# Two-operand clamps on the vector engine, unit heads and square sums later in a slot, the rotary sum at a slot's end, and one layer norm of GpSimd a slot later

## The chip, the cores and the metric

The kernel runs on one NeuronCore of a Trainium2 chip. The metric is the device time of one launch in microseconds. A core has five engines that run at the same time, each with its own program in a fixed order: TensorE (PE, matrix products and transposes), VectorE (DVE), ScalarE (ACT), GpSimd (POOL) and SyncE (SP, which issues the DMA transfers here). They meet only at semaphores. PE writes its results to PSUM; POOL reads and writes SBUF alone.

## The reference, cut to what matters

There are 16 sequences of 512 tokens of width 128. Each goes through a first attention (16 heads of width 8, interleaved rotary, causal softmax) behind a layer norm, and then through a block of two layers with token shift, local attention (8 heads of width 64, windows of 64) and a gated MLP.

```
x = x + attn_ref(layernorm(x), wq, wk, wv, wo)
x = x + ffn_ref(layernorm(x), ...)
# each of the two layers in ffn_ref:
q = l2norm(q) * qs ; k = l2norm(k) * ksc      # t / clip(norm(t), 1e-12)
q, k = rotary_xpos(q, k)
o = local_attention(q, k, v) ; x = x + o @ wo
h = shift_token(x)
h = (h - mu) / sqrt(var + 1e-05) * lg + lb
a, g = split(h @ w1 + b1) ; x = x + (a * gelu(g)) @ w2 + b2
```

The clip of the norm is the clamp that the change touches: the kernel takes the maximum of the sum of squares and 1e-24 and then raises it to the power -0.5. The other clamp-like step is the addition of 1e-5 to a variance.

## The kernel before, in words

**Rounds and slots.** Two sequences ("lanes") are a pair, and there are 8 pairs. A round `i` has 16 slots `s`. In a slot the five engines work on a tile of 128 tokens of the two-layer block (`ITEMS` = 2 layers x 2 lanes x 4 tiles = 16 per round, so 128 tiles in all), on two heads of the first attention of a later pair, and on small parts of two other stages: the projections of the pair after next ("next") in slots 0 to 6 for one lane and 8 to 14 for the other, and the end of the first attention of the next pair ("first"). The program is written out slot by slot: rounds -2 and -1 fill the pipeline (no tiles of the block), rounds 0 to 5 hold everything, round 6 has no "next" stage, round 7 has tiles only, and a short tail follows. Every engine's list of one slot is the `for s in slots` loop at the end of its section; nothing reorders it.

**One tile.** PE projects q and k, three slots ahead (`project_qk(s + 3)`, L699). ACT copies them to `RAW` and squares them (`SQ`). DVE sums the squares per head and clamps the sum: `norms(s + 3)`, L1029 and L1032, in place in `ss`. POOL raises `ss` to the power -0.5 (`over_norms(s + 2)`, L1408, result `inv`), multiplies `RAW` by the rotary tables (L1386, and L1397 twice) and adds the two (`added`, L1403). DVE multiplies by `inv`: `unit_heads(s + 1)`, L1012, result `QN`. PE turns `QN` (`turn_qk`), computes the scores of tile `s` (L725 is their first product, so it marks the start of a slot on PE), DVE takes the maxima (L1019, L1022), ACT the exponentials, PE the values (L751), DVE divides by the sums (`over_sums(s)`, L1036 and L1039, result `ON`), PE merges with `wo` (L786), DVE adds to the stream `Z` (`add_heads(s - 1)`, L1048), and `tile_moments(s - 1)` ends with L1066, the variance plus 1e-5 (`veps`), from which POOL takes the root (L1378) and normalises (L1417).

**Waits between DVE and POOL.** `over_norms(s + 2)` waits for `unit_heads(s + 1)` of the same slot (`qn_ready`), because `RC` and `inv` are single buffers. `norms(s + 3)` waits for `over_norms(s + 2)` of the same slot (`inv_ready`), because `ss` is a single buffer. `scores(s + 1)` on PE waits for `ON` of tile `s`.

**Six steps of the first attention.** In each slot PE, DVE and ACT pass six `attention_step`s (positions 0 to 5), for two heads of three chunks. DVE takes row maxima (L977). The bank of PSUM is single, so PE's scores of step n (L587) wait for DVE's maximum of step n - 1: what stands between two steps on DVE can hold up PE.

**The MLP.** In even slots DVE multiplies the gates (`gate_up`, L1076), PE projects down (L828), DVE adds (`add_mlp`, L1084), and in the second layer also adds the kept input (`XR`, L1089). In slots 4, 6, 8 and 10 PE then turns the result (`turn_half`), which waits for L1084.

**POOL's other work.** At the start of an even slot it splits the maxima (`maxima_parts`, L1367 to L1373), for which PE's L622 waits in that slot. `next_normalise` (L1348, L1342) stands at the start of slots 1 and 9, ahead of `over_norms`. `first_normalise` (L1354, L1342) of lane 1 stands at the start of slot 15, that of lane 0 at the end of slot 7. SP reloads `X1` (`load_first`) once the latter is through.

Of the kernel before, what the change touches and what calls it, by code (L numbers as in the profile page):

```python
# [21 lines left out]
P = 128  # L22
B, S, D = 16, 512, 128
NT = S // P
# [146 lines left out]
def build(nc, t, out):  # L171
    with ExitStack() as ctx:
# [28 lines left out]
        lgb = sb("lgb", [P, L, 2])  # L201
        nhalf = sb("nhalf", [P, 2 * H2])
        spare = sb("spare", [P, 1])
        unit1 = sb("unit1", [P, 1])
# [183 lines left out]
        N_FIRST, N_CONST = 4, 10 + L * 7  # L388
        N_MADE = LANES + 9

# [7 lines left out]
        def _(sp):  # L398
# [31 lines left out]
            def body(i, slots):  # L430
# [69 lines left out]
                for s in slots:  # L500
# [11 lines left out]
                    for z in range(LANES):  # L512
# [4 lines left out]
                        if s == 7 + 8 * z and lives(i, 1):  # L517
                            keep_first(1, z)
                    if s == 8 and lives(i, 1):
                        sp.wait_ge(*past(ln_out.sem[0], ln_out.at(later(i, 1), 1)))  # L520
                        load_first(1, 1)
# [394 lines left out]
        def _(v):  # L916
# [3 lines left out]
            def moments(k, z, src, to, counted, meant, done):  # L920
                stats, mv, veps = to
                for tt in range(NT):
                    ins = v.bn_stats(stats[:, tt, :], src[:, tt, :])
                ins.then_inc(counted.sem[z], 1)
                v.wait_ge(*past(counted.sem[z], counted.at(k, 1)))
                v.tensor_copy(spare[:, 0:1], nhalf[:, 0:1])
                for tt in range(NT):
                    ins = v.bn_aggr(mv[:, tt, :], stats[:, tt, :])
                ins.then_inc(meant.sem[z], 1)
                v.wait_ge(*past(meant.sem[z], meant.at(k, 1)))  # L930
                v.tensor_scalar(veps[:, :], mv[:, :, 1], EPS, None, ALU.add).then_inc(done.sem[z], 1)

# [10 lines left out]
            def next_sin(n, z, w):  # L943
                if w:
                    v.wait_ge(*past(parts.sem[z], parts.at(n, w)))
                v.wait_ge(*past(proj.sem[z], proj.at(n, 2 * w + 2)))
                v.tensor_tensor(rope_s[:, :], a_ps, sin1[:, :], ALU.mult).then_inc(roped.sem[z], 1)
                v.wait_ge(*past(roped.sem[z], roped.at(n, 2 * w + 2)))
                v.tensor_tensor(rope_t[:, :], rope_t[:, :], rope_s[:, :], ALU.add).then_inc(rope_sum.sem[z], 1)
# [20 lines left out]
            def body(i, slots):  # L970
# [55 lines left out]
                def norms(m):  # L1026
                    v.wait_ge(*past(sq_done.sem, sq_done.at(i, m + 1)))
                    v.wait_ge(*past(inv_ready.sem, inv_ready.at(i, m)))
                    v.tensor_reduce(ss[:, :], SQ.rearrange("p (h e) -> p h e", e=E2), AX.X,  # L1029
                                    ALU.add).then_inc(ss_sum.sem, 1)  # L1030
                    v.wait_ge(*past(ss_sum.sem, ss_sum.at(i, m + 1)))
                    v.tensor_scalar(ss[:, :], ss[:, :], 1e-24, None, ALU.max).then_inc(ss_ready.sem, 1)  # L1032

# [26 lines left out]
                def tile_moments(m):  # L1060
# [4 lines left out]
                    v.wait_ge(*past(tile_mean.sem, tile_mean.at(i, m + 1)))  # L1065
                    v.tensor_scalar(veps[z][:, tt:tt + 1], mv[z][:, tt, 1:2], EPS, None,  # L1066
                                    ALU.add).then_inc(tile_var.sem, 1)
# [23 lines left out]
                for s in slots:  # L1091
# [4 lines left out]
                    if isinstance(i, int) and i == -2 and s == 7:  # L1096
                        scale_tables()
                    if tile_in(i, s):
                        maxima(s)
                    attention_step(s, 0)  # L1100
                    if tile_in(i, s + 1):
                        unit_heads(s + 1)
                    if s % 8 == 4 and lives(i, 2):
                        next_cos(two, z, 1)
                        next_low(two, z, 0)
                    if s % 8 == 6 and lives(i, 2):
                        next_low(two, z, 1)
                    attention_step(s, 1)
                    if tile_in(i, s - 1):
                        add_heads(s - 1)  # L1110
                    attention_step(s, 2)
                    if s % 8 == 3 and lives(i, 2):
# [5 lines left out]
                    attention_step(s, 3)  # L1118
                    if tile_in(i, s + 3):
                        norms(s + 3)  # L1120
                    if tile_in(i, s - 1):
                        shifted_tokens(s - 1)
                    if b:
                        gate_up(p, 0)
                        gate_up(p, 1)
                    if s % 2 and unit_in(i, (s + 17) // 2):
                        heads_over_sum((s + 17) // 2)
                    if tile_in(i, s - 1):
                        tile_moments(s - 1)
# [14 lines left out]
                    if s % 8 == 2 and lives(i, 2):  # L1144
                        next_sin(two, z, 0)
                    if s % 8 == 6 and lives(i, 1):
                        add_attention(one, z)
# [178 lines left out]
        def _(g):  # L1326
# [8 lines left out]
            g.memset(unit1[:, :], 1.0).then_inc(made, 1)  # L1335
            g.memset(nhalf[:, :], -0.5).then_inc(made, 1)
            g.wait_ge(made, N_MADE)

# [20 lines left out]
            def body(i, slots):  # L1359
# [62 lines left out]
                for s in slots:  # L1422
# [16 lines left out]
                    if tile_in(i, s - 1):  # L1439
                        tile_normalise(s - 1)  # L1440
                    if s == 7 and lives(i, 1):
                        first_normalise(later(i, 1), 0)
# [73 lines left out]
```

## Time and profile before

| | |
|---|---|
| Median of 3 runs | 2443.89 us (2443.87 to 2459.32) |
| Profiled execution | 2439.99 us, of which the span is 2438.2 us |
| PE, matrix products | busy 2153.6 us (88%) |
| DVE | busy 1763.4 us (72%) |
| ACT | busy 1553.0 us (64%) |
| POOL | busy 1773.9 us (73%) |
| DMA | 49 GB/s over the span |

How to read it: busy is the time in which an engine has at least one instruction under way. Matrix products overlap each other, so a busy PE can hold waits that don't show as idle. No engine is near the whole span, so the order of the lists and the waits between them decide, and the trace of waits and the timeline are of more use than the shares. Times in the rows are microseconds from the start of the span unless marked ns.

### The profile page before, as it was taken

The numbers are of one execution on the slowest core, as the hardware profiler recorded it, in microseconds if no ns is written. First come the engines' busy times: TensorE is split into PE (matmuls) and PEld (weight loads), VectorE is DVE, ScalarE is ACT, GpSimd is POOL, SyncE is SP. The second block draws the span as 40 slices with busy tenths as digits, with TensorE's granted clock in tenths as the row PEclk, the third lists the DMA queues.
The fourth block names the chain that finished last, engine by engine and source line by source line (L and its number), as shares of the span: only waits on it lengthen the run. The fifth ranks groups of instructions, "written<-read, shape, count | busy, mean of one in ns | idle before, by whom it ended". The sixth has DMA issues, their size and how long they took to land.

```text
span 2438.2 us, 55022 instructions
## 1 busy us (share of the span) xinstructions
PE 2153.6 (88%) x20736; PEld 1447.8 (59%) x20736; DVE 1763.4 (72%) x4632; ACT 1553.0 (64%) x2510; POOL 1773.9 (73%) x1615
## 2 busy tenths in 40 slices
PE   4887899899999989998999999999899999988886
PEld 1444566665666666665666656666566666665654
DVE  4766777787777877788777777778777777666653
ACT  1445666676676667666766766766676667765553
POOL 2126768787777868787686777878787778788882
PEclk9999999999999999999999999999999999999997
DMA  4222121121212111121112112121121211111110
GB/s 138 65 66 54 40 53 49 44 59 45 57 37 60 52 46 49 48 59 46 49 49 59 44 45 58 33 64 51 39 51 47 60 48 36 25 32 27 28 25 23
DMA packets 115081, 119.56 MB, mean 49 GB/s; under 512 B 31945, under 2 KB 88054, under 8 KB 114818
## 3 DMA queue, kind: packets, MB, share of 16 engines
q1 hardware_dynamic: 114818, 116.04, 18.2%
q8 instruction: 167, 2.74, 0.5%
q14 instruction: 96, 0.79, 0.1%
HBM read 55.96 MB, written 20.97 MB: 32 GB/s over the span
## 4 chain that ended last, share of the span: by engine, by line
PE 38%; DVE 21%; ACT 14%; POOL 13%; issue 11%; DMA 1%; SPq 1%; ACTq 0%; DVEq 0%; POOLq 0%
PE ps L734 4%; PE ps L645 4%; POOL inv L1408 4%; DVE ps L977 4%; PE ps L554 4%; PE ps L828 3%; DVE nm L1019 3%; PE ps L587 3%; DVE ss L1029 3%; PE ps L712 3%; PE ps L600 2%; PE ps L567 2%; ACT PT L1190 2%; PE ps L810 2%; PE ps L819 2%
## 5 line engine op out<-in xcount | busy, mean ns | idle before, releaser
L977 DVE CUSTOM_DVE_ANT_0 ps<-ps,causal 128x512 f32<-128x512 f32 (+3 forms) x1024 | 492.4, 506 | 328.3 <-PE ps L587 322.3
L1408 POOL TENSOR_TENSOR inv<-ss,nhalf 128x16 f32<-128x16 f32 x128 | 377.7, 2950 | 394.0 <-DVE QN L1012 394.0
L1190 ACT ACTIVATE PT<-ps 128x512 f32<-128x512 f32 (+1 forms) x768 | 409.1, 536 | 352.5 <-PE ps L602 349.8
L587 PE MATMUL ps<-KA,QA 72*128 72x512 bf16 (+3 forms) x1024 | 275.1, 311 | 77.1 <-DVE nmax L977 72.9
L1397 POOL TENSOR_TENSOR RS<-RAW,rot 128x512 f32<-128x512 f32 x256 | 319.9, 1271 | 0.0
L1403 POOL TENSOR_TENSOR RC<-RC,RS 128x1024 f32<-128x1024 f32 x128 | 300.9, 2351 | 18.4
L600 PE MATMUL ps<-QA,KA 75*128 75x512 bf16 (+3 forms) x1024 | 286.8, 306 | 27.8 <-ACT PT L1190 26.0
L1386 POOL TENSOR_TENSOR RC<-RAW,rot 128x1024 f32<-128x1024 f32 x128 | 307.9, 2405 | 0.0
L1019 DVE TENSOR_REDUCE nm<-ps 128x8 f32<-128x1024 f32 x128 | 156.4, 1222 | 119.3 <-PE ps L734 119.3
L699 PE MATMUL ps<-wqkv,ZT 128*128 128x512 f32 x512 | 241.9, 595 | 0.0
L587 PEld LDWEIGHTS ps<-KA,QA 72*128 72x128 bf16 x1024 | 96.4, 100 | 235.3 <-DVE nmax L977 142.4
L1249 ACT COPY V_odd<-ps 128x512 f32<-128x512 f32 x128 | 75.0, 586 | 233.6 <-PE ps L712 232.1
L1029 DVE TENSOR_REDUCE ss<-SQ 128x16 f32<-128x1024 f32 x128 | 155.7, 1217 | 72.5 <-POOL inv L1408 65.5
L602 PE MATMUL ps<-causal_t,identb 128*128 128x128 bf16 x1024 | 200.9, 222 | 0.0
L1225 ACT ACTIVATE PX<-PX 128x1024 f32<-128x1024 f32 x128 | 136.5, 1067 | 54.8 <-DVE PX L1022 54.1
L600 PEld LDWEIGHTS ps<-QA,KA 75*128 75x128 bf16 x1024 | 101.0, 99 | 115.8 <-ACT PT L1190 64.7
L645 PE MATMUL ps<-PT,V 128*32 128x512 f32 (+3 forms) x2048 | 153.4, 440 | 9.1 <-DVE X L1003 2.9
L1022 DVE TENSOR_TENSOR PX<-ps,nm 128x1024 f32<-128x1024 f32 x128 | 156.7, 1224 | 4.4
L1012 DVE TENSOR_TENSOR QN<-RC,inv 128x1024 f32<-128x1024 f32 x128 | 156.5, 1223 | 0.0
L828 PE MATMUL ps<-w,G 128*128 128x128 f32 (+1 forms) x768 | 110.8, 297 | 44.8 <-DVE G L1076 44.8
L734 PEld LDWEIGHTS ps<-KT,QT 64*64 64x64 f32 x4096 | 114.3, 136 | 56.7 <-issue 56.7
L751 PE MATMUL ps<-V_even,PT 128*64 128x65 f32 x2048 | 147.2, 225 | 0.4
(122 smaller groups left out, 5304.9 us busy)
## 6 DMA issues: line engine op xcount, KB each, us to landing
V_even<-V_odd SPq DMA_DIRECT2D x256, 130.0 KB, 2.6
QA<-parts SPq DMA_DIRECT2D x192, 96.0 KB
KA<-parts SPq DMA_DIRECT2D x192, 96.0 KB
parts<-qkp SPq DMA_DIRECT2D x32, 384.0 KB, 3.5
X_next<-in_x SPq DMA_DIRECT2D x16, 256.0 KB, 3.1
X<-in_x SPq DMA_DIRECT2D x16, 256.0 KB, 2.9
x_kept<-X SPq DMA_DIRECT2D x16, 256.0 KB, 3.8
XR<-x_kept SPq DMA_DIRECT2D x32, 128.0 KB, 2.9
```

Of the source, the lines that this page charges most:

```text
L587: last = pe.matmul(dst[:, c0:c0 + w], QA[e][0:QK_ROWS, h % UNIT, qt * P:(qt + 1) * P], KA[e][0:QK_ROWS, h % UNIT, 0:w], start=True, stop=True)
L600: pe.matmul(dst[:, c0:c0 + w], KA[e][0:ROWS, h % UNIT, kt * P:(kt + 1) * P], QA[e][0:ROWS, h % UNIT, kt * P:S], start=True, stop=False)
L645: last = pe.matmul(a_ps[32 * n:32 * (n + 1), kt * P:S], V1[z][:, kt, h * VW:h * VW + 32], PT1[:, n, c0:c0 + w], start=(kt == 0), stop=(kt ...
L699: mm = pe.matmul(ps[:, w, :], ZT[z][:, tt * P:(tt + 1) * P], wqkv[:, l, w * INNER:(w + 1) * INNER], start=True, stop=True)
L977: ins = v.tensor_tensor_reduce(for_max(i, x)[:, c0:c0 + w], for_max(i, x)[:, c0:c0 + w], causal[:, S - w:S], -1.0, -NEG, ALU.add, ALU.min, ...
L1019: v.tensor_reduce(nm[:, :], blocks, AX.X, ALU.max, negate=True).then_inc(max_ready.sem, 1)
L1029: v.tensor_reduce(ss[:, :], SQ.rearrange("p (h e) -> p h e", e=E2), AX.X, ALU.add).then_inc(ss_sum.sem, 1)
L1190: a.activation(PT1[:, h % UNIT, c0:c0 + w], for_exp(i, x)[:, 0:w], ACT.Exp, scale=SCALE1).then_inc(exped.sem, 1)
L1386: g.tensor_tensor(RC.rearrange(heads, w=2, h=H2), RAW[m % 2].rearrange(heads, w=2, h=H2), rot[:, l, tt, 0, :, :].unsqueeze(2).to_broadcast ...
L1397: ins = g.tensor_tensor(turned[:, w, :, :, :], by_half[:, w, :, :, :], table[:, w, :, :].unsqueeze(1).to_broadcast([P, H2, 2, E2 // 2]), A ...
L1403: g.tensor_tensor(RC, RC, RS, ALU.add).then_inc(added.sem, 1)
L1408: g.tensor_tensor(inv[:, :], ss[:, :], nhalf[:, :], ALU.pow).then_inc(inv_ready.sem, 1)
```

## The change

**Two operands instead of a constant.** Two small tables are filled once by POOL: `tiny` (1e-24, 128x16) and `eps` (1e-5, 128x4). The clamp L1032 and the additions of 1e-5 (L1066, L931) were `tensor_scalar` with a constant; they are `tensor_tensor` with the table as the second operand.

**Order of DVE's list.** `unit_heads(s + 1)` moves from behind step 0 to behind step 1 and `add_heads`. `norms(s + 3)` moves from behind step 3 to behind the gates and `heads_over_sum`. `shifted_tokens` moves with it. In slots 4 and 12 the product by the cosines (`next_cos`, lane w = 1) moves to the very start of the slot and `next_low` behind step 2. The sum of the two rotary products (L949) is a function of its own, at the end of slots 2, 4, 10 and 12; in slots 4 and 12 it stood right behind the product by the sines.

**POOL and SP.** `first_normalise` of lane 0 moves from the end of slot 7 to the end of slot 8, and SP's reload of `X1` from slot 8 to slot 10.

```diff
-                v.tensor_scalar(veps[:, :], mv[:, :, 1], EPS, None, ALU.add).then_inc(done.sem[z], 1)
+                v.tensor_tensor(veps[:, :], mv[:, :, 1], eps[:, :], ALU.add).then_inc(done.sem[z], 1)
...
                 v.tensor_tensor(rope_s[:, :], a_ps, sin1[:, :], ALU.mult).then_inc(roped.sem[z], 1)
+
+            def next_sum(n, z, w):
                 v.wait_ge(*past(roped.sem[z], roped.at(n, 2 * w + 2)))
...
-                    v.tensor_scalar(ss[:, :], ss[:, :], 1e-24, None, ALU.max).then_inc(ss_ready.sem, 1)
+                    v.tensor_tensor(ss[:, :], ss[:, :], tiny[:, :], ALU.max).then_inc(ss_ready.sem, 1)
...
-                    v.tensor_scalar(veps[z][:, tt:tt + 1], mv[z][:, tt, 1:2], EPS, None,
+                    v.tensor_tensor(veps[z][:, tt:tt + 1], mv[z][:, tt, 1:2], eps[:, 0:1],
...
+                    if s % 8 == 4 and lives(i, 2):
+                        next_cos(two, z, 1)
                     if tile_in(i, s):
                         maxima(s)
                     attention_step(s, 0)
+                    attention_step(s, 1)
+                    if tile_in(i, s - 1):
+                        add_heads(s - 1)
                     if tile_in(i, s + 1):
                         unit_heads(s + 1)
+                    attention_step(s, 2)
                     if s % 8 == 4 and lives(i, 2):
-                        next_cos(two, z, 1)
                         next_low(two, z, 0)
                     if s % 8 == 6 and lives(i, 2):
                         next_low(two, z, 1)
-                    attention_step(s, 1)
-                    if tile_in(i, s - 1):
-                        add_heads(s - 1)
-                    attention_step(s, 2)
...
-                    if tile_in(i, s + 3):
-                        norms(s + 3)
-                    if tile_in(i, s - 1):
-                        shifted_tokens(s - 1)
                     if b:
                         gate_up(p, 0)
                         gate_up(p, 1)
                     if s % 2 and unit_in(i, (s + 17) // 2):
                         heads_over_sum((s + 17) // 2)
+                    if tile_in(i, s + 3):
+                        norms(s + 3)
+                    if tile_in(i, s - 1):
+                        shifted_tokens(s - 1)
...
                         next_sin(two, z, 0)
+                        next_sum(two, z, 0)
+                    if s % 8 == 4 and lives(i, 2):
+                        next_sum(two, z, 1)
...
-                    if s == 7 and lives(i, 1):
+                    if s == 8 and lives(i, 1):
                         first_normalise(later(i, 1), 0)
```

The rows below show three places in the programs of both kernels, all in round 2. Behind the edits the changed kernel's line numbers are 2 to 10 higher (L977 is L981 there, L1012 is L1016, L1408 is L1418); the second row of each L977 reads the accumulator.

DVE, slot 10, from step 0 on, before:

```order
L977 ISA ps,nmax<-ps,causal 128x512
L977 ISA nmax 128x1
L1012 TENSOR_TENSOR QN<-RC,inv 128x1024
L977 ISA ps,nmax<-ps,causal 128x384
L977 ISA nmax 128x1
L977 ISA ps,nmax<-ps,causal 128x128
L977 ISA nmax 128x1
L1048 TENSOR_TENSOR Z<-ps,Z 128x128
```

The same place in the changed kernel:

```order
L981 ISA ps,nmax<-ps,causal 128x512
L981 ISA nmax 128x1
L981 ISA ps,nmax<-ps,causal 128x384
L981 ISA nmax 128x1
L981 ISA ps,nmax<-ps,causal 128x128
L981 ISA nmax 128x1
L1052 TENSOR_TENSOR Z<-ps,Z 128x128
L1016 TENSOR_TENSOR QN<-RC,inv 128x1024
```

`QN` stood behind the first maximum and now stands behind the next two (step 1 has two) and behind the addition to `Z`.

DVE, slot 10, from step 3 to `veps`, before:

```order
L977 ISA ps,nmax<-ps,causal 128x512
L977 ISA nmax 128x1
L1029 TENSOR_REDUCE ss<-SQ 128x16
L1032 TENSOR_SCALAR ss<-ss 128x16
L1058 BN_STATS stats<-XN 128x6
L1076 SCALAR_TENSOR_TENSOR G<-ps,b,G 128x256 x2
L1063 COPY spare<-nhalf 128x1
L1064 BN_AGGR mv<-stats 128x2
L1066 TENSOR_SCALAR veps<-mv 128x1
```

The same place in the changed kernel:

```order
L981 ISA ps,nmax<-ps,causal 128x512
L981 ISA nmax 128x1
L1080 SCALAR_TENSOR_TENSOR G<-ps,b,G 128x256 x2
L1033 TENSOR_REDUCE ss<-SQ 128x16
L1036 TENSOR_TENSOR ss<-ss,tiny 128x16
L1062 BN_STATS stats<-XN 128x6
L1067 COPY spare<-nhalf 128x1
L1068 BN_AGGR mv<-stats 128x2
L1070 TENSOR_TENSOR veps<-mv,eps 128x1
```

The gates come first now, then the sum of squares and the clamp, which reads a second tensor, then the moments, whose last row reads a second tensor too.

POOL, from the end of slot 7 to the start of slot 8's `inv`, before:

```order
L1378 TENSOR_TENSOR rstd<-veps,nhalf 128x1
L1414 TENSOR_TENSOR pool_spare<-nhalf 128x1
L1417 TENSOR_SCALAR XN<-Z,mv,rstd 128x64
L1417 TENSOR_SCALAR XN<-XN,mv,rstd 128x64
L1354 TENSOR_TENSOR first_rstd<-first_veps,nhalf 128x4
L1340 TENSOR_TENSOR pool_spare<-nhalf 128x1
L1342 TENSOR_SCALAR Z_first<-X,first_mv,first_rstd 128x128 x4
L1367 TENSOR_TENSOR nparts<-nmax,unit 128x4x4
L1369 TENSOR_TENSOR nres<-nmax,nparts 128x4x4
L1371 TENSOR_TENSOR nparts<-nres,unit 128x4x4
L1373 TENSOR_TENSOR nparts<-nres,nparts 128x4x4
L1408 TENSOR_TENSOR inv<-ss,nhalf 128x16
```

The changed kernel, from the end of slot 8 to slot 9's `inv`:

```order
L1388 TENSOR_TENSOR rstd<-veps,nhalf 128x1
L1424 TENSOR_TENSOR pool_spare<-nhalf 128x1
L1427 TENSOR_SCALAR XN<-Z,mv,rstd 128x64
L1427 TENSOR_SCALAR XN<-XN,mv,rstd 128x64
L1364 TENSOR_TENSOR first_rstd<-first_veps,nhalf 128x4
L1350 TENSOR_TENSOR pool_spare<-nhalf 128x1
L1352 TENSOR_SCALAR Z_first<-X,first_mv,first_rstd 128x128 x4
L1358 TENSOR_TENSOR rstd_next<-veps_next,nhalf 128x4
L1350 TENSOR_TENSOR pool_spare<-nhalf 128x1
L1352 TENSOR_SCALAR XN_next<-X_next,mv_next,rstd_next 128x128 x4
L1418 TENSOR_TENSOR inv<-ss,nhalf 128x16
```

The layer norm into `Z_first` now stands directly ahead of the one into `XN_next`, both ahead of slot 9's `inv`; in slot 8 `nparts` no longer has it in front.

## Rows read from the trace of the kernel before

**Rows 1.** Waits of all engines: engine, line, releaser, us in total, times, longest:

```profile
POOL inv L1408 <- DVE QN L1012: 394.0, 92, 8.6
...
PEld ps L587 <- DVE nmax L977: 142.4, 145, 4.7
...
DVE ss L1029 <- POOL inv L1408: 65.5, 34, 5.4
...
PE ps L828 <- DVE G L1076: 44.8, 40, 3.8
...
PE ps L622 <- POOL nparts L1373: 17.7, 10, 4.0
```

**Rows 2.** Groups of instructions, the clamp: busy us, mean ns; idle before:

```profile
L1032 DVE TENSOR_SCALAR ss<-ss 128x16 f32<-128x16 f32 x128 | 119.3, 932 | 4.4
```

**Rows 3.** Single lines of DVE: duration ns min/median/max, first and last start:

```profile
L1032 DVE TENSOR_SCALAR ss<-ss x128: 175/878/3462, 192.8 to 2364.7; 128x16 f32<-128x16 f32 x128
...
L949 DVE TENSOR_TENSOR rope_t<-rope_t,rope_s x32: 691/693/2332, 23.5 to 1870.2; 128x512 f32<-128x512 f32 x32
...
L1066 DVE TENSOR_SCALAR veps<-mv x128: 153/154/156, 252.8 to 2418.1; 128x1 f32<-128x1 f32 x128
```

**Rows 4.** Timeline of slot 4, DVE and POOL: start us, duration us, instruction:

```profile
871.53 2.33 DVE L949 TENSOR_TENSOR rope_t<-rope_t,rope_s 128x512 f32<-128x512 f32 x1
...
870.96 2.35 POOL L1403 TENSOR_TENSOR RC<-RC,RS 128x1024 f32<-128x1024 f32 x1
```

**Rows 5.** Timeline, DVE and POOL, a product beside the power and L1386:

```profile
318.58 0.69 DVE L953 TENSOR_TENSOR rope_s<-rope_t,qkp 128x512 f32<-128x512 f32 x1
...
316.00 2.92 POOL L1408 TENSOR_TENSOR inv<-ss,nhalf 128x16 f32<-128x16 f32 x1 [8.53 <-DVE QN L1012]
318.89 2.60 POOL L1386 TENSOR_TENSOR RC<-RAW,rot 128x1024 f32<-128x1024 f32 x1
```

**Rows 6.** Timeline of round 2, PE: starts of slots 0, 1 and 8 to 11:

```profile
788.02 0.38 PE L725 MATMUL ps<-band,identb 128*128 128x512 bf16 x1
...
802.92 0.59 PE L725 MATMUL ps<-band,identb 128*128 128x512 bf16 x2
...
929.47 0.59 PE L725 MATMUL ps<-band,identb 128*128 128x512 bf16 x2
...
946.93 0.59 PE L725 MATMUL ps<-band,identb 128*128 128x512 bf16 x2
...
964.41 0.59 PE L725 MATMUL ps<-band,identb 128*128 128x512 bf16 x2
...
980.84 0.59 PE L725 MATMUL ps<-band,identb 128*128 128x512 bf16 x2
```

**Rows 7.** Timeline of slot 10, DVE, then POOL:

```profile
969.11 1.22 DVE L1012 TENSOR_TENSOR QN<-RC,inv 128x1024 f32<-128x1024 f32 x1
...
971.09 0.29 DVE L1048 TENSOR_TENSOR Z<-ps,Z 128x128 f32<-128x128 f32 x1
...
974.24 1.22 DVE L1029 TENSOR_REDUCE ss<-SQ 128x16 f32<-128x1024 f32 x1
975.49 0.27 DVE L1032 TENSOR_SCALAR ss<-ss 128x16 f32<-128x16 f32 x1
...
978.50 0.69 DVE L1039 TENSOR_TENSOR ON<-ps,rec 128x512 f32<-128x512 f32 x1
...
970.47 2.92 POOL L1408 TENSOR_TENSOR inv<-ss,nhalf 128x16 f32<-128x16 f32 x1 [2.07 <-DVE QN L1012]
973.36 2.36 POOL L1386 TENSOR_TENSOR RC<-RAW,rot 128x1024 f32<-128x1024 f32 x1
975.69 2.50 POOL L1397 TENSOR_TENSOR RS<-RAW,rot 128x512 f32<-128x512 f32 x2
```

**Rows 8.** Timeline of POOL in slot 9, the next pair's layer norm ahead of `inv`:

```profile
949.94 1.03 POOL L1348 TENSOR_TENSOR rstd_next<-veps_next,nhalf 128x4 f32<-128x4 f32 x1
...
955.23 2.92 POOL L1408 TENSOR_TENSOR inv<-ss,nhalf 128x16 f32<-128x16 f32 x1
```

More of the change, by code:

```diff
@@ L202, in build @@
         nhalf = sb("nhalf", [P, 2 * H2])
+        tiny = sb("tiny", [P, 2 * H2])
+        eps = sb("eps", [P, NT])
         spare = sb("spare", [P, 1])
@@ L388, in build @@
         N_FIRST, N_CONST = 4, 10 + L * 7
-        N_MADE = LANES + 9
+        N_MADE = 2 * LANES + 9
         def past(sem, value):
@@ L518, in body @@
                             keep_first(1, z)
-                    if s == 8 and lives(i, 1):
+                    if s == 10 and lives(i, 1):
                         sp.wait_ge(*past(ln_out.sem[0], ln_out.at(later(i, 1), 1)))
@@ L1336, in _ @@
             g.memset(nhalf[:, :], -0.5).then_inc(made, 1)
+            g.memset(tiny[:, :], 1e-24).then_inc(made, 1)
+            g.memset(eps[:, :], EPS).then_inc(made, 1)
             g.wait_ge(made, N_MADE)
```

## The prediction

> **What bounds the kernel now.** I read the waits first. PE waits for DVE in two places: its scores L587 for the row maxima L977 (142.4 us on the weight side), and its down projection L828 for the gates (44.8 us) [rows 1]. DVE waits for POOL's power `inv` 34 times (65.5 us), and POOL waits 394.0 us for DVE's `QN` [rows 1]. So POOL has air (some 3 us per slot) and starts each tile only when DVE says so; DVE is late at some places and early at others; PE carries most of the span. Then the groups and the single lines: DVE's clamp L1032 of 16 columns takes 932 ns on average, 119.3 us in all [rows 2], but 175 ns at its shortest and 3462 ns at its longest [rows 3]. The work is the same each time, so the rest, 119 - 128 x 0.175 = 97 us, is waiting inside the instruction. The timeline says for what. In slot 10 the clamp ran from 975.49 to 975.76 and POOL's L1386 from 973.36 to 975.72 [rows 7]: it ended 0.04 us behind POOL's instruction. L1066 does almost the same on one column and never takes more than 156 ns [rows 3].
>
> **Does a two-operand form escape that wait?** This decides the case. The trace has no clamp with two tensors, but it has L949, a sum of two f32 tensors in SBUF: 691 ns at best, 2332 at worst [rows 3]. One of 2.33 us began at 871.53, 0.57 us into POOL's L1403, which ended at 873.31; L949 ended at 873.86 [rows 4], 0.55 behind it, so it did its 0.69 us of work only from about 0.14 before POOL's end on. With 0.175 us of work and the same start, a two-tensor clamp would end 0.035 behind POOL's instruction, just where the one-tensor clamp ends now. The other bound is L953, also two SBUF tensors (one bf16), which took its plain 0.69 us beside L1408; but L1408 is the power, and the next L1386, which met the end of L953, took 2.60 us instead of 2.36 [rows 5, 7]. So between 0 and -97 us of DVE time for L1032, I take 0: the POOL instructions that it meets are L1386 and L1397, products like L1403 and not powers. And L1066, which now never waits, becomes a two-tensor instruction. It follows 0.45 us behind L1032, when POOL runs L1397: cost 0 if it stays exempt, up to one L1397 (1.25 us) if not. I take that it waits.
>
> The Trainium skill says the same more sharply ("SBUF — State Buffer", section "Who interferes with whom"): a DVE instruction with two SBUF inputs contends with a GpSimd instruction that reads SBUF. By it the clamp gains nothing and L1066 loses. Rows 4 agree with it.
>
> **The moved steps.** What counts is how late `QN` becomes, since `inv` waits for `QN`, the sum of squares waits for `inv`, and on DVE's list the clamp, `veps`, step 4, `ON` and with it PE's next slot stand behind the sum of squares.
>
> In slot 10 before: `QN` ends at 970.33, `inv` runs 970.47 to 973.39, L1029 starts at 974.24 (0.85 of slack), `ON` ends at 979.19, PE starts slot 11 at 980.84 [rows 6, 7]. After: `QN` stands behind L1048, which waits for PE's merge and ends at 971.38. `QN` ends at 972.5, 2.2 later. From there the chain is:
> - `inv`: 0.15 + 2.92;
> - L1029, 0.05 behind `inv`: 1.22. The clamp then meets L1386 (2.36) and ends with it, 2.39 behind the end of `inv`;
> - 0.45 of moments; `veps` meets the first L1397 (1.25) and ends with it, 3.65 behind the end of `inv`;
> - the two maxima of step 4, 0.75 and, in slots 2 and 10, 0.6 of L941; `ON`: 0.2 + 0.7.
>
> Sum 0.15 + 2.92 + 3.65 + 0.75 + 0.95 = 8.4 from the end of `QN` to `ON`. `QN` ends 972.5 - 964.4 = 8.1 behind PE's slot start, so an even slot lasts at least 16.5 to 16.6 us, an odd one (its `QN` comes some 1.6 later, behind PE's values) at least 18.2. Before, slot 0 lasted 802.92 - 788.02 = 14.9, slot 10 16.4, slot 8 17.46, slot 9 17.48 [rows 6].
>
> Per round, in us, by that floor: slot 0 +1.7; slot 2 +0.9; slot 10 +1.5 (with L941 and the turn behind `add_mlp`, 0.9); odd slot 7 +1.1; slots 3, 5, 11, 13 are long already and change by 0. Slots 4 and 12 gain: today L957, L941 and `QN` hold up step 1, and L949's stretch (2.33, of which 1.64 is waiting [rows 3, 4]) holds up step 4. Both go; the floor takes the rest of it: -1.0 and -1.3. In slots 6 and 14 the gates no longer wait for the clamp: +0.1 and -0.7. Slot 1 loses its 3.46 us clamp but sits on the floor: -0.9.
>
> **POOL's layer norm.** In slot 8 it no longer stands ahead of `nparts`, for which PE waits about 2 us there (17.7 us in ten waits [rows 1]); but slot 8's floor (16.6 + 0.9) equals its 17.46 of today: 0. In slot 9 the two norms come back to back. One costs 955.23 - 949.94 = 5.3 us [rows 8]. POOL is done with slot 8 at 949.9 as today (its `QN` was POOL-bound there), then 4.5 and 4.5 to 5.4 more: `inv` starts at about 959.5 instead of 955.2, `ON` ends about 8.3 later, and PE starts slot 10 at 967.9 instead of 964.41: +3.5. Slot 15 has a norm ahead of `inv` behind a slot 14 that now ends later on POOL: +1.9. DMAs: SP issues the same ones, the reload of `X1` two slots later is needed only in slot 14 and landed in about 3 us; nothing.
>
> Sum per round: 1.7 - 0.9 + 0.9 - 1.0 + 0.1 + 1.1 + 0 + 3.5 + 1.5 - 1.3 - 0.7 + 1.9 = +6.8, times six full rounds = +41. Round 6 has shorter slots: +1.6 on most even ones, less slot 8, +1.1 on six odd ones: +13. Round 7: the gates, for which L828 waits there (44.8 us in all [rows 1]), come earlier, but the same chain ends even slots where they end now (+0.2 each), odd ones +1.1: +10. Total +64 on 2440 of the profiled execution, 2504; that execution is 4 us below the median of the runs, and I round to **2500**.
>
> **Rivals.**
> 1. *The two-tensor forms don't wait at all* (small tensors, as L953 beside the power). Then the clamp saves 0.8 to 1.0 and `veps` costs nothing: the chain is 1.7 shorter. Slots 0, 2, 7, 10 come back to 0, slots 4 and 12 gain about 3 each, 6 and 14 1.3 each, 1 gains 1.7, 8 gains 1.6, 9 still loses 3.7, 15 is even: about -8 per round, -48, and some -12 behind: **2380**. For it: nothing in the trace but rows 5. This one is on the other side. It decides as soon as the chain from `QN` to `ON` is under 6.8 us.
> 2. *L1032 waits, the one-column L1066 stays exempt*, as its one-column form is now. The chain is 0.8 shorter; that lifts some 12 slots of a full round and 15 each of the last two: 64 - 6 x 9.6 - 24 = -18, about **2425**, and with the slack left in some of these slots anything up to 2460. No difference that counts.
> 3. *DVE loses its turn.* Where the clamp began just behind `inv`, with about 1 us of L1386 left, POOL's next product sometimes went first, three times in a row (the 3462 ns [rows 3]; it happened 7 times, nearly all in slot 1). After the change nearly every clamp begins at that phase. If one in five is lost, 128 x 0.2 x 2.2 = +56 more: **2560**.
>
> **Chances.** The forecast 0.45, rival 1 0.17, rival 2 0.23, rival 3 0.15. About 1% (24 us) is what a measurement of this kernel can tell from none. Slower by over 1%: 0.45 + 0.15 = 0.60; faster: rival 1 and a part of rival 2, 0.20; between: 0.20. The forecast's own range is 2470 to 2540, the whole 2405 to 2560, which leaves out most of rival 1 and the far end of rival 3.
>
> **What would show it.** L1032's mean stays near or above 0.9 us (rival 1: 0.18). L1066's mean goes from 0.154 to 0.5 or more (rival 2: stays). DVE's wait for `inv` grows well over 65.5 us, and DVE gets a busy time near today's or above. PE starts slot 10 of round 2 over 3 us later after slot 9 began than now. L949's maximum falls to about 0.7. I am wrong if the clamp is short beside L1386, or if DVE reaches the sum of squares behind the end of `inv` in most slots.

## The result, and the profile after

The changed kernel took 2500.61 us (median of 4 runs, 2497.22 to 2522.69), the kernel before 2447.55 us (4 runs). The ratio is 1.0225, with a 95% interval of 1.0182 to 1.0268: slower by about 2%; the medians are 53 us apart. The prediction said 2500 and slower.

The page of the changed kernel, its span and busy times (us, share, number of instructions):

```profile
span 2495.9 us, 55024 instructions
...
PE 2172.9 (87%) x20736; PEld 1438.3 (58%) x20736; DVE 1860.5 (75%) x4632; ACT 1550.4 (62%) x2510; POOL 1740.5 (70%) x1617
```

DVE is busy for 97 us more with exactly as many instructions. Its waits (engine, line, releaser: us in total, times, longest):

```profile
POOL inv L1418 <- DVE QN L1016: 510.3, 119, 8.6
...
PEld ps L589 <- DVE nmax L981: 179.6, 234, 7.4
...
DVE ss L1033 <- POOL inv L1418: 91.9, 78, 6.0
```

Against [rows 1], POOL waits 116 us more for `QN`, 119 times instead of 92; DVE waits for `inv` 78 times instead of 34; and PE's score products wait for DVE's maxima 37 us more. The single lines of DVE in the changed kernel (duration in ns, min/median/max):

```profile
L1036 DVE TENSOR_TENSOR ss<-ss,tiny x128: 176/1011/3455, 184.4 to 2428.3; 128x16 f32<-128x16 f32 x128
...
L1070 DVE TENSOR_TENSOR veps<-mv,eps x128: 158/733/1991, 243.8 to 2476.9; 128x1 f32<-128x1 f32 x128
...
L953 DVE TENSOR_TENSOR rope_t<-rope_t,rope_s x32: 677/692/1114, 23.0 to 1912.2; 128x512 f32<-128x512 f32 x32
```

The clamp got no shorter (median 1011 ns, 878 in [rows 3]). The step that never waited, 154 ns in [rows 3], now takes 733. The rotary sum lost its 2.33 us stretch: at most 1.11 us now.

The timeline of slot 10 of round 2 in the changed kernel (start us, duration us; in brackets the idle time before and what ended it), the place of [rows 7]. DVE, then POOL:

```profile
983.70 1.22 DVE L1016 TENSOR_TENSOR QN<-RC,inv 128x1024 f32<-128x1024 f32 x1
...
988.09 1.22 DVE L1033 TENSOR_REDUCE ss<-SQ 128x16 f32<-128x1024 f32 x1 [0.71 <-POOL inv L1418]
989.34 1.03 DVE L1036 TENSOR_TENSOR ss<-ss,tiny 128x16 f32<-128x16 f32 x1
...
990.85 0.73 DVE L1070 TENSOR_TENSOR veps<-mv,eps 128x1 f32<-128x1 f32 x1
...
993.05 0.69 DVE L1043 TENSOR_TENSOR ON<-ps,rec 128x512 f32<-128x512 f32 x1
...
985.06 2.92 POOL L1418 TENSOR_TENSOR inv<-ss,nhalf 128x16 f32<-128x16 f32 x1 [3.29 <-DVE QN L1016]
987.95 2.39 POOL L1396 TENSOR_TENSOR RC<-RAW,rot 128x1024 f32<-128x1024 f32 x1
990.28 2.51 POOL L1407 TENSOR_TENSOR RS<-RAW,rot 128x512 f32<-128x512 f32 x2
```

The clamp ends at 990.37, 0.03 behind L1396 (990.34). The row of L1407 holds two products; `veps` ends at 991.58, behind the first of them. `QN` ends at 984.92 and `ON` at 993.74: the chain is 8.8 us long. DVE now stands idle 0.71 us before the sum of squares, where before it came 0.85 late.

The granted clock by slot, PE alone (stretch in us, its length, PE busy and its instructions, granted clock, DMA share, GB/s). Slots 1, 9 and 10 of round 2 before the change:

```profile
802.92:822.37 19.45, 17.40 (x177) 1.00 0.27 66
...
946.93:964.40 17.47, 16.99 (x176) 1.00 0.14 33
964.40:980.84 16.44, 15.93 (x153) 1.00 0.24 66
```

The same slots in the changed kernel, then slot 9 of round 3, then slot 1 of round 1:

```profile
810.60:830.33 19.73, 18.95 (x175) 0.91 0.17 39
...
956.42:976.81 20.39, 18.37 (x177) 0.94 0.12 32
976.81:994.69 17.88, 16.27 (x152) 1.00 0.26 70
...
1246.85:1272.06 25.21, 17.79 (x177) 0.88 0.17 46
...
518.61:537.37 18.76, 17.26 (x175) 1.00 0.18 42
```

Where the 58 us between the two profiled executions (2438.2 and 2495.9 us) lie, by PE's slot starts: up to the first slot of round 0 -9; rounds 0 to 5 +47; round 6 +19; round 7 with the tail +1.

### The profile page after: what moved, and what is told of

Read it like the earlier page. It is cut to its first block, busy times and chain, and to the rows that moved or that the text cites. A ratio compares the mean times of both kernels' runs of the same rounds, so it can differ in the third digit from the quotient of the medians.

```text
span 2495.9 us, 55024 instructions
## 1 busy us (share of the span) xinstructions
PE 2172.9 (87%) x20736; PEld 1438.3 (58%) x20736; DVE 1860.5 (75%) x4632; ACT 1550.4 (62%) x2510; POOL 1740.5 (70%) x1617
## 3 DMA queue, kind: packets, MB, share of 16 engines
q1 hardware_dynamic: 114818, 116.04, 17.3%
## 4 chain that ended last, share of the span: by engine, by line
PE 33%; DVE 31%; POOL 17%; ACT 10%; issue 8%; DMA 1%; SPq 1%; DVEq 0%; POOLq 0%; ACTq 0%
POOL inv L1418 12%; PE ps L736 5%; PE ps L647 5%; DVE ss L1033 5%; DVE QN L1016 5%; DVE ps L981 5%; DVE ss L1036 4%; PE ps L788 4%; PE ps L701 3%; PE ps L589 3%; DVE nm L1023 3%; DVE PX L1026 3%; PE ps L727 3%; PE ps L556 2%; PE ps L602 2%
## 5 line engine op out<-in xcount | busy, mean ns | idle before, releaser
L1418 POOL TENSOR_TENSOR inv<-ss,nhalf 128x16 f32<-128x16 f32 x128 | 374.4, 2925 | 510.3 <-DVE QN L1016 510.3
L981 DVE CUSTOM_DVE_ANT_0 ps<-ps,causal 128x512 f32<-128x512 f32 (+3 forms) x1024 | 490.2, 503 | 198.0 <-PE ps L589 195.8
L1407 POOL TENSOR_TENSOR RS<-RAW,rot 128x512 f32<-128x512 f32 x256 | 319.2, 1270 | 0.0
L1413 POOL TENSOR_TENSOR RC<-RC,RS 128x1024 f32<-128x1024 f32 x128 | 302.2, 2361 | 18.6 <-POOL RS L1407 0.4
L1396 POOL TENSOR_TENSOR RC<-RAW,rot 128x1024 f32<-128x1024 f32 x128 | 303.0, 2367 | 0.0
L647 PE MATMUL ps<-PT,V 128*32 128x512 f32 (+3 forms) x2048 | 159.8, 454 | 24.4 <-issue 15.7
L1016 DVE TENSOR_TENSOR QN<-RC,inv 128x1024 f32<-128x1024 f32 x128 | 155.5, 1215 | 0.2 <-issue 0.2
L736 PEld LDWEIGHTS ps<-KT,QT 64*64 64x64 f32 x4096 | 120.5, 142 | 58.3 <-issue 58.3
L736 PE MATMUL ps<-KT,QT 64*64 64x128 f32 x4096 | 153.9, 292 | 0.0
```

Of the source, the lines that this page charges most:

```text
L647: last = pe.matmul(a_ps[32 * n:32 * (n + 1), kt * P:S], V1[z][:, kt, h * VW:h * VW + 32], PT1[:, n, c0:c0 + w], start=(kt == 0), stop=(kt ...
L736: mm = pe.matmul(ps[b * WIN:(b + 1) * WIN, 2 + s, j * P:(j + 1) * P], QT[half, j, b * WIN:(b + 1) * WIN], keys, start=False, stop=j == PAI ...
L981: ins = v.tensor_tensor_reduce(for_max(i, x)[:, c0:c0 + w], for_max(i, x)[:, c0:c0 + w], causal[:, S - w:S], -1.0, -NEG, ALU.add, ALU.min, ...
L1396: g.tensor_tensor(RC.rearrange(heads, w=2, h=H2), RAW[m % 2].rearrange(heads, w=2, h=H2), rot[:, l, tt, 0, :, :].unsqueeze(2).to_broadcast ...
L1407: ins = g.tensor_tensor(turned[:, w, :, :, :], by_half[:, w, :, :, :], table[:, w, :, :].unsqueeze(1).to_broadcast([P, H2, 2, E2 // 2]), A ...
L1413: g.tensor_tensor(RC, RC, RS, ALU.add).then_inc(added.sem, 1)
```

## The experiments

Ratios are to the kernel before on the same chip, timed in the same session (2435.9 to 2437.0 us there). Kernels of different sessions are compared by their ratios: so the changed kernel's 1.0225 against e5's 1.0040 is 1.85%, 45 us. The two intervals together leave some 12 us on either side of such a difference. "Per round" is the mean of rounds 2 to 5 of the profiled execution: 284.9 us before, 292.7 changed.

**e1, the changed kernel with constants again** (all three lines; the cut shows two, one of them without the line that it replaces).

```diff
-                    v.tensor_tensor(ss[:, :], ss[:, :], tiny[:, :], ALU.max).then_inc(ss_ready.sem, 1)
+                    v.tensor_scalar(ss[:, :], ss[:, :], 1e-24, None, ALU.max).then_inc(ss_ready.sem, 1)
...
+                    v.tensor_scalar(veps[z][:, tt:tt + 1], mv[z][:, tt, 1:2], EPS, None,
```

> The changed kernel with the constant forms back (clamp and both additions of 1e-5), all moves kept. Theory A (late inv with waits): the clamp stays at about 1.0 us, since the constant form waits for POOL's product just as the two-operand form does; the one-column addition falls from 0.73 to 0.15 us, which shortens the chain from QN to ON by 0.58 in some 12 slots of a full round: 12 x 0.58 x 6 = 42 us, with round 6 about 50, so about 2450. Theory B (only the moves count): 2500.

2442.06 us, ratio 1.0032 [1.0013, 1.0051]; per round 286.7. Nearly the whole loss is gone, and the clamp's row reads as in the changed kernel:

```profile
L1036 DVE TENSOR_SCALAR ss<-ss x128: 174/1006/3433, 187.1 to 2375.9; 128x16 f32<-128x16 f32 x128
```

**e5, only `veps` back on a constant.**

> The changed kernel with only the per-tile variance step (veps, 128x1) back on a constant; the clamp keeps its two operands. Theory A (what the two-operand forms cost is almost all in the one-column veps, held up beside POOL's L1407 in every slot; the clamp waits the same either way): veps back to 0.154 us, 128 x 0.58 us shorter on the chain, ratio to the kernel before 1.003 +- 0.005 as in e1_constants, about 2445 us, clamp mean still near 1.04 us. Theory B (the two-operand clamp costs too, by lost turns or a longer hold): about half way, ratio 1.012, 2470 us.

2443.27 us, ratio 1.0040 [1.0015, 1.0066], equal to e1 within their intervals (8 us). So the two-operand clamp costs and saves nothing that shows; the one-column step carries the loss, some 45 us. In its row of the e5 kernel it takes its own time again:

```profile
L1070 DVE TENSOR_SCALAR veps<-mv x128: 153/154/155, 247.2 to 2442.7; 128x1 f32<-128x1 f32 x128
```

Most of the slots that got shorter in e1 and e5 lost 0.6 us, but slots 3 and 15 got 0.6 and 0.8 longer. The addition to `XR` (L1093) at the end of the slots before them has two SBUF inputs as well. When it begins earlier, it waits longer for the end of POOL's sum L1413: ahead of slot 15 of round 2 it ended 0.28 us behind that in the changed kernel and 0.29 in e1. Its row in the changed kernel, then in e1:

```profile
L1093 DVE TENSOR_TENSOR XR<-XR,Z x32: 424/1394/1987, 447.4 to 2493.2; 128x256 f32<-128x256 f32 x32
...
L1093 DVE TENSOR_TENSOR XR<-XR,Z x32: 425/1986/2601, 451.3 to 2437.7; 128x256 f32<-128x256 f32 x32
```

**e2, the kernel before with the two-operand forms alone.**

> The kernel before with the two-operand forms only, no move. Theory A: the clamp keeps its mean of about 0.93 us; the one-column addition finds POOL's product with 0.08 us left in even slots (nothing) and 0.37 left in odd ones (0.24 us more), so within 10 us of before, 2445 to 2458. If the operand forms alone were the cause: about 2500. If two operands escaped the wait: clamp 0.18 us and a faster kernel.

2471.96 us, ratio 1.0135 [1.0066, 1.0205]: a miss, 36 us where under 10 were expected. The four runs fall into two groups, 2458 to 2460 and 2484 to 2487 us (+22 to +51); the profiled one (2484.10) belongs to the upper, so what follows tells of that. In the order of before `veps` comes when POOL's second L1397 (L1401 here) has little left, so it takes 0.38 us at the median. But the clamp sometimes begins while POOL's L1390 (L1386 before) is under way and comes back only behind POOL's next two products. I call that a lost turn. There were 11 in this execution and 7 before, and each now costs twice, since `veps` then meets the sum L1407 (1.63 to 1.65 us behind each of the 11). Timeline of e2, slot 1 of round 2, DVE, then POOL:

```profile
827.60 3.47 DVE L1034 TENSOR_TENSOR ss<-ss,tiny 128x16 f32<-128x16 f32 x1
...
831.90 1.64 DVE L1068 TENSOR_TENSOR veps<-mv,eps 128x1 f32<-128x1 f32 x1
...
826.21 2.37 POOL L1390 TENSOR_TENSOR RC<-RAW,rot 128x1024 f32<-128x1024 f32 x1
828.55 2.49 POOL L1401 TENSOR_TENSOR RS<-RAW,rot 128x512 f32<-128x512 f32 x2
831.18 2.34 POOL L1407 TENSOR_TENSOR RC<-RC,RS 128x1024 f32<-128x1024 f32 x1
```

The clamp ends 0.03 behind the second L1401, and `veps` 0.02 behind L1407. Slot 1 grew by 1.7 us, slot 2 behind it by 1.0 (its clock in round 2 was 0.93).

**e3, `unit_heads` back behind step 0 in the changed kernel.**

```diff
                     attention_step(s, 0)
+                    if tile_in(i, s + 1):
+                        unit_heads(s + 1)
                     attention_step(s, 1)
                     if tile_in(i, s - 1):
                         add_heads(s - 1)
-                    if tile_in(i, s + 1):
-                        unit_heads(s + 1)
```

> The changed kernel with unit_heads back behind step 0, all else kept. Theory A: inv starts 2 to 3 us earlier, so DVE no longer waits for it in slots 0, 2, 7, 10 and those of round 6: the sum of squares starts off the phase right behind inv. 4 to 5 us per full round and 15 in round 6 come back: 2450 to 2465. If the lateness of QN does not matter: 2500.

2436.32 us, ratio 1.0006 [0.9981, 1.0031]; per round 285.6. The direction was right, the size larger than expected: undoing this edit alone also takes away the whole loss, 53 us by the ratios. The full rounds gave 7 us each for the 4 to 5 expected, round 6 12 for 15, and round 7 with the tail 20 for nothing.

**e9, the kernel before with `unit_heads` later and nothing else.**

> The kernel before with unit_heads behind step 1 and add_heads as its only edit. Theory A (the prediction's chain: QN some 2 us later makes inv, the sum of squares and ON later in most slots; e3_heads_back won 7 us per round by undoing it): +4 to +7 us per round, less in slots 4 and 12 where the rotary steps hold PE up anyway; 2465 to 2485 us, ratio 1.012 to 1.020. Theory B (it costs only together with the held veps): ratio under 1.005, 2445 us.

2579.98 us, ratio 1.0578 [1.0540, 1.0615]. Both theories were far too small: 143 us. The waits of e9 name what both had left out:

```profile
DVE ss L1029 <- POOL inv L1408: 207.6, 119, 5.1
PEld ps L828 <- DVE G L1076: 141.2, 63, 4.2
```

In the order of before the gates stand behind the sum of squares. When `QN` is late, so is `inv`; DVE stops at the sum of squares, and the gates stop with it. Slot 10 of round 2 in e9, DVE:

```profile
1026.56 1.22 DVE L1029 TENSOR_REDUCE ss<-SQ 128x16 f32<-128x1024 f32 x1 [1.44 <-POOL inv L1408]
...
1028.87 0.85 DVE L1076 SCALAR_TENSOR_TENSOR G<-ps,b,G 128x256 f32<-128x256 f32 x2
```

Behind that wait PE's clock falls. The same slot of e9, PE, in its last four stretches of 2 us, and the slot as a whole:

```profile
1027.00:1029.00 2.00, 0.99 (x32) 1.00 0.15 51
1029.00:1031.00 2.00, 1.23 (x11) 1.00 0.46 111
1031.00:1033.00 2.00, 2.00 (x7) 0.56 0.35 119
1033.00:1035.00 2.00, 2.00 (x7) 0.58 0.07 22
...
1015.28:1035.13 19.85, 17.56 (x151) 0.91 0.22 59
```

The slot took 16.44 us before, with PE busy for 15.93. Of the 3.4 us that it grew, 1.6 are PE's busy time, the same work at the lower level of its clock. Round 4 shows the price by itself: the wait for the gates was the same 1.78 us, the clock stayed at 1.00, and the slot took 18.15 us:

```profile
1615.40:1633.55 18.15, 15.85 (x152) 1.00 0.24 62
```

Slot 8 has a second wait. With the later `QN` POOL reaches the layer norm at the end of slot 7 later, and PE waits 4.1 us for `nparts`, 1.9 before. The changed kernel has neither wait: PE waited for the gates only at the very end (0.97 us, twice) and in slot 8 of no full round for `nparts`. So the new place of the gates and that of the layer norm take away what makes the later `QN` so dear in e9. No run has the later `QN` with one of the two alone, so how the difference divides between them is not shown.

**e4, the kernel before with the rotary moves alone** (`next_cos` first, `next_low` behind step 2, the sum at the slot's end).

> The kernel before with the rotary moves only (product by the cosines first in slots 4 and 12, residual low parts behind step 2, sum at the slot's end). Theory A: slots 4 and 12 lose the 1.64 us wait of the sum and the hold-up of step 1 (about 1.1), slots 6 and 14 about 0.6: 4 to 5 us per full round, 2415 to 2425. If those waits were covered: 2447.

2368.89 us, ratio 0.9732 [0.9695, 0.9770]; per round 273.7, 11.2 less where 4 to 5 were expected. Slots 4 and 12 went from 19.3 and 18.6 us to 15.7 and 15.8, 6 and 14 from 17.6 and 17.3 to 16.0 and 15.8, and slot 1 lost 2.0, since its clamp lost its turn in one round of six instead of in all of them. In each of these four even slots PE is idle for only 0.5 us now.

**e7, e4 with the sum of squares and `shifted_tokens` behind the gates.**

> The kernel before with the rotary moves of e4_rotary_only and, in addition, the sum of squares and clamp behind the gates. Theory A (the later sum of squares costs nothing, since the sum of squares waits for inv anyway, and PE's wait for the gates in slots 0 and 8, 0.65 and 0.87 us, goes): -1 to -1.5 us per round against e4_rotary_only, about 2360 us, ratio 0.970. Theory B (each 0.9 us by which the clamp is later makes the next slot's inv and ON late): +6 or more per round, 2400 us or more, ratio 0.985 or more.

2365.19 us, ratio 0.9719 [0.9695, 0.9743]. That can't be told from e4; theory B falls. It holds two opposite things: full rounds are 2.0 us longer (in slot 8 PE waits 0.7 to 1.2 us for `Z`), and round 7 with the tail is 14 us shorter (233.4 for 247.5), where the gates come earlier.

**e6, the layer norm back in slot 7 of the changed kernel.**

> The changed kernel with the first layer norm of lane 0 back at the end of slot 7 and SP's reload of X1 back in slot 8. Theory A (slot 9's 21.7 us comes from two layer norms back to back ahead of inv): slot 9 falls to about 18, slot 8 gets PE's wait for nparts back (about 1.9 us, before it 1.0 of its floor), sum -2 to -3 per round, about 2480 us, ratio 1.013 to 1.017. Theory B (slot 9 is long because QN comes late anyway): slot 9 stays over 20.5 us, 2495 to 2505 us, ratio 1.022.

2525.95 us, ratio 1.0376 [1.0348, 1.0404]. Slot 9 got shorter, as theory A said (3.3 us), but the sum has the other sign, so neither theory holds. The slots 8 and 9 of round 2 in e6, and POOL in slot 8:

```profile
953.47:976.18 22.71, 16.12 (x146) 0.92 0.22 59
976.18:994.26 18.08, 17.30 (x176) 1.00 0.07 17
```

```profile
958.68 3.74 POOL L1352 TENSOR_SCALAR Z_first<-X,first_mv,first_rstd 128x128 f32<-128x128 f32 x4
962.39 0.21 POOL L1377 TENSOR_TENSOR nparts<-nmax,unit 128x16 bf16<-128x16 f32 x1
```

With the later `QN` POOL reaches the norm later, so PE's wait for `nparts` is 3.5 us instead of the 1.9 before, and slot 8 lasts 22.7 us, against 17.5 with the norm moved (where PE never waits for `nparts`). Moving it takes 5.2 us out of slot 8 and puts 3.3 into slot 9. Of the 26 us between the two profiled spans 14 lie in rounds 0 to 5, 5 in round 6 and 5 before round 0; by the ratios it is 37 us.

**e8, e4 with a clamp that takes one SBUF operand.** The maximum is a reduction over pairs (sum, 1e-24); the result is the same.

```diff
-                    v.tensor_reduce(ss[:, :], SQ.rearrange("p (h e) -> p h e", e=E2), AX.X,
+                    v.tensor_reduce(pair[:, :, 0], SQ.rearrange("p (h e) -> p h e", e=E2), AX.X,
...
-                    v.tensor_scalar(ss[:, :], ss[:, :], 1e-24, None, ALU.max).then_inc(ss_ready.sem, 1)
+                    v.tensor_reduce(ss[:, :], pair[:, :, :], AX.X, ALU.max).then_inc(ss_ready.sem, 1)
```

> e4_rotary_only with the clamp written as a maximum over pairs (sum, 1e-24) by a tensor_reduce, that is one SBUF input of 128x32 and no constant; same result. Theory A (what holds the clamp is the kind of operand access, and an instruction with one plain SBUF input runs beside POOL's product): the clamp takes its own 0.2 us in all 128 tiles instead of 0.77 on average, no lost turns; since even slots of e4_rotary_only have no stall left, it gives time in slots 9, 13 and 15 and in the last two rounds, 2345 to 2360 us, ratio 0.963 to 0.970. Theory B (anything DVE starts there waits for POOL's product): clamp mean stays near 0.77, 2369 us, ratio 0.973.

2353.07 us, ratio 0.9668 [0.9648, 0.9688]. The clamp in e8, and in slot 10 beside POOL's L1394 (L1386 before), DVE, then POOL:

```profile
L1035 DVE TENSOR_REDUCE ss<-pair x128: 185/186/189, 189.9 to 2282.3; 128x16 f32<-128x32 f32 x128
```

```profile
945.04 0.19 DVE L1035 TENSOR_REDUCE ss<-pair 128x16 f32<-128x32 f32 x1
...
942.91 2.37 POOL L1394 TENSOR_TENSOR RC<-RAW,rot 128x1024 f32<-128x1024 f32 x1
```

It began 0.24 us before POOL's product ended and did not wait for it, and in no tile took over 0.189 us. Theory A holds: the kind of instruction decides, not the moment. It is 0.6% under e4, its interval just clear of e4's; e10 prices the clamp more clearly.

**e10, this clamp as the only edit of the kernel before.**

> The kernel before with the pair clamp of e8_pair_clamp as its only edit. It prices a clamp that never waits. Theory A (of the 97 us of waiting in the clamp only the lost turns, 3.46 us in slot 1, and some in slots 8 and 15 lie on the path): clamp 0.186 us in all tiles, slot 1 down by 1 to 2 us, the other slots by under 0.5, -2 to -3.5 us per round, 2415 to 2425 us, ratio 0.990 to 0.995. Theory B (rival 1 of the prediction: most of it is on the path): 2390 us or less, ratio 0.98 or less.

2397.54 us, ratio 0.9834 [0.9811, 0.9857]: 39 us, between the two theories. Slot 1 gave 1.5 us, slots 6, 14 and 15 0.9 each (in slot 15 all of it is one lost turn, in round 3), and round 7 with the tail 12 (242.6 for 254.4): there the clamp had waited 0.8 us in each of 13 tiles, 10.5 us together, so about all of it lay on the path.

**e11, e8 with the sum of squares behind the gates, and e12, e8 with the layer norm in slot 8.**

> e8_pair_clamp with the sum of squares behind the gates as well. Theory A (with a clamp that never waits the later sum of squares costs nothing and PE's wait for the gates in slots 0 and 8, 0.4 us each, goes): 2345 to 2352 us, ratio 0.963 to 0.967. Theory B (PE's wait for Z in slot 8, 1.1 us in e7, comes here too): 2355 to 2362 us, ratio 0.968 to 0.971.

> e8_pair_clamp with the first layer norm of lane 0 at the end of slot 8 and SP's reload of X1 in slot 10. Theory A (the prediction's step: slot 8 loses PE's wait for nparts, 2.07 us, and slot 9 with two norms back to back gains 2 to 4 us): 2350 to 2365 us, ratio 0.966 to 0.971. Theory B (as in the changed kernel, where the slot of the norm was worth 26 us): 2330 to 2340 us, ratio 0.957 to 0.961.

e11: 2334.34 us, ratio 0.9575 [0.9556, 0.9594], the fastest kernel here, 4% under the one before and below both ranges. Full rounds are as long as in e8; of the 19 us between the two profiled spans, 11.5 lie in round 7 and 6.6 before round 0. e12: 2346.57 us, ratio 0.9625 [0.9604, 0.9647]. Slot 8 lost 2.7 us, slots 9 and 10 gained 3.1, so the rounds came out even, as theory A had it. The total fell by 0.4%, more than it said; 7.8 us of it lie before round 0.

## Why the prediction was right, and where it was not

The direction, the mechanism of the forms and the chain held. That the number came within 1 us is luck: terms of both signs cancelled, as told below, and the rounding helped. The sum of +64 on the median before, 2443.89, gives 2508; the prediction took it on the profiled 2440 and rounded down.

**The forms.** Both steps held. The clamp gains nothing (its row is the same in both forms, and e1 equals e5), and the one-column `veps` begins to wait. It took 0.73 us and not up to 1.25, because it began when L1407 had already run for half a microsecond. Its price came from two terms, 64 + 18 = 82 us between the forecast and rival 2; e5 measured 45, so this term was nearly twice too large. The wait was 0.58 us where 0.8 was taken, and part of what a short `veps` gives back goes into the longer wait of the addition to `XR` (slots 3 and 15 in e5), which no row had been read for. Rival 1 falls by the rows of L1036. Rival 2 falls by those of L1070. Rival 3, lost turns, fell too: 2 of 128 in the changed kernel's profiled execution for the one in five that it took, although 127 clamps began at the phase feared. It was right as a mechanism, as e2 shows (11 turns), but the phase alone doesn't decide it. The count also changes between executions: e5's profiled one, the slowest of its ten (2463.70 us, median 2443.27), had six at the same phase, and its slot 9 took 23.4 us in each of the five rounds with one, 20.8 in e1 without.

**The chain.** 8.4 us were worked out from the end of `QN` to `ON`; slot 10 shows 8.8. `QN` was put 8.1 us behind PE's slot start and ends 8.1 behind it. Slot 10 grew by 1.8 us (+1.5), slot 0 by 1.3 (+1.7), slot 7 by 1.0 (+1.1), slot 2 by 0.6 (+0.9), slot 15 by 1.4 (+1.9); slots 4, 12 and 14 lost 1.5, 1.5 and 0.9 (-1.0, -1.3, -0.7). Rounds 0 to 5 gave +47 for +41.

**Four steps that failed inside a right sum.**
- Slot 1: +0.3 for -0.9. The clock was missing from the sum. It was 1.00 there before and is 0.91 in rounds 2 to 5, where PE's busy time rose from 17.40 to 18.95 us for the same work. In round 1 the clock stayed at 1.00, and the slot took 18.76 us, 0.7 less than before, near the forecast.
- Slot 9: +4.3 for +3.5. Round 3, with a lost turn and a clock of 0.88, took 25.2; the other three grew by 3.1 on average (2.9 in round 2, where the prediction's sign asked for over 3). So the term was near and a little large, though its clock of 0.87 to 0.94 stood in no sum either.
- Slot 3: +1.2 for 0, and slot 15, near its +1.9 for another reason than the one given. In both PE's value product L647 waits for a step of DVE at the end of the slot before (1.1 and 1.7 us): the product by the sines, and the addition of the attention to `X`. Both stand behind the addition to `XR`, and no row had been read for them. For slot 15 the prediction blamed POOL's layer norm ahead of `inv`, but POOL stood idle 2.28 us there, waiting for `QN`. The rows of round 2, first around the start of slot 3 (DVE, PE), then around that of slot 15 (DVE, POOL, PE):

```profile
847.67 1.39 DVE L1093 TENSOR_TENSOR XR<-XR,Z 128x256 f32<-128x256 f32 x1
...
849.33 0.68 DVE L949 TENSOR_TENSOR rope_s<-ps,sin 128x512 f32<-128x512 f32 x1
...
850.11 2.36 PE L647 MATMUL ps<-PT,V 128*32 128x512 f32 x32 [1.10 <-issue]
...
1065.44 1.99 DVE L1093 TENSOR_TENSOR XR<-XR,Z 128x256 f32<-128x256 f32 x1
...
1067.70 0.68 DVE L1007 TENSOR_TENSOR X<-ps,X 128x512 f32<-128x512 f32 x1
...
1064.80 2.35 POOL L1413 TENSOR_TENSOR RC<-RC,RS 128x1024 f32<-128x1024 f32 x1
...
1076.79 2.92 POOL L1418 TENSOR_TENSOR inv<-ss,nhalf 128x16 f32<-128x16 f32 x1 [2.28 <-DVE QN L1016]
...
1068.48 2.36 PE L647 MATMUL ps<-PT,V 128*32 128x512 f32 x32 [1.70 <-issue]
```

- Round 7: +1 for +10, and round 6 +19 for +13. "The same chain ends even slots where they end now" left out that the gates set them too: before the change PE waited for them in the even slots of round 7, now it doesn't. Against the changed kernel, e5 is 10 us shorter there and e3 20; the gates first gave 14 in e7. These large terms of both signs cancel.

**What the sum hid.** The prediction added small differences per slot and found +7 per round. The runs show that the edits are neither small nor additive: the whole is +53. On the kernel before, the rotary moves alone are worth -67 us, the forms +36 and the heads +143. In the changed kernel, undoing the forms gives 47 and undoing the heads 53. So the heads, which the prediction priced only as a floor under each slot, are the worst edit. What saves them, by the waits that e9 has and the changed kernel has not, is that the gates now stand ahead of the sum of squares and the layer norm out of `nparts`' way. The prediction charged the layer norm's move with 3.5 us per round. Against slot 9 of before that was about right, but the edit itself is a gain in this company (e6 is 1.5% slower without it): the zero for slot 8 came from comparing with a slot whose `QN` was early, and with the later `QN` the norm in front makes `nparts` late.

**The time before round 0.** It fell by 9 us, which no step foresaw. Part of it seems to be the layer norm's move, which acts in the two filling rounds too: the five kernels with it reach round 0 at 211.8 to 217.4 us, the nine without it at 214.5 to 223.5, and the two pairs that differ in nothing else show 5.4 and 7.8 us. That isn't all of it: e11, which doesn't have the move, reaches round 0 6.6 us earlier than e8. The rest is not settled.

## What to carry to other kernels

A two-operand form doesn't free a small DVE instruction from waiting for GpSimd, and it can make one wait that was free; a reduction over pairs does free it, if the constant can lie beside the value (1.7% here by itself, in e10). Before moving a step later, look at what stands behind the wait that it delays: a late `QN` cost 143 us with the gates behind the waiting instruction, and 53 in a kernel that has the gates ahead of it and a layer norm out of the way. A sum over slots can be right while its terms are not, so try each edit alone, and undo each one in the whole.

## What the runs showed of the hardware

- One column is enough. A `TENSOR_TENSOR` of 128x1 f32 with both inputs in SBUF waits for the end of GpSimd's product (0.73 us and up to 1.99 for 0.158 of work); the same step with a constant took 0.153 to 0.156 us before the change and in e1 and e5, where it begins beside the same product. With 16 columns both forms wait alike.
- A `TENSOR_REDUCE` from SBUF did not wait in any tile: 0.185 to 0.189 us with 128x32 in e8, and 1.21 to 1.22 us for the sum of squares of 128x1024 before the change and after. The Trainium skill says so ("SBUF — State Buffer", section "Who interferes with whom": a reduction never contends, two SBUF inputs do); the rows of e8 and of L1070 agree. One thing here goes against it: beside the power of 128x16 (`inv`), which reads SBUF too, the two-input steps L957 and L961 took their plain 0.68 to 0.69 us in all 47 cases of the changed kernel. So what counts is the GpSimd instruction too, as the prediction took from [rows 5].
- DVE can lose its turn: 3.4 to 3.5 us with about 1 us left of GpSimd's product, 3.1 us with 0.6 left. In the changed kernel 127 of 128 tiles began with 0.95 to 1.00 us left, and only two lost their turn. What decides it is open.
- The granted clock falls to its lower level (1.2 for 2.4 GHz) behind some of PE's stalls. In e9's slot 10, 4 us in which PE was busy for 2.2 were followed by 4 us at 0.56 to 0.58; waits of 1.1 to 2.6 us for the gates in every even slot of a full round went with a mean clock of 0.951 in that execution, against 0.980 before. Not every such stall is followed by a fall: round 4 of e9's slot 10, with the same wait, kept 1.00 and was 1.7 us shorter. So a stall can be paid twice.
